# A two-layer decoder on one core: the five written orders of its steps are permuted

## The reference

```python
x = _layernorm(x + _L0_attn_ref(x, q, k, v, o))         # linear attention, 16 heads of 16
x = _layernorm(x + _L0_xattn_ref(x, ids, ctx))          # 4 experts over ctx, chosen by token id
x = _layernorm(x + _L0_ffn_ref(x, Wg, Wu, Wd, Wr))      # 8 gated experts, "golden" weights
x = _layernorm(x + _L1_attn_ref(x, Wq, Wk, Wv))         # softmax in groups of 32 tokens, half the heads rolled
x = _layernorm(x + _L1_xattn_ref(x, ctx, mask))         # attention over ctx with a pad mask
x = _layernorm(x + _L1_ffn_ref(x, gate, gate_up, down)) # 8 experts, top 2, and a shared one
```

## Time and profile before

| | us |
|---|---|
| median of 3 runs | 436.18 |
| lowest, highest | 435.44, 438.01 |
| the profiled execution | 438.25 |
| its span | 436.3 |
| TensorE (PE) busy | 417.6 |
| POOL, DVE, ACT busy | 275.3, 260.0, 242.8 |
| mean granted TensorE clock | 0.989 |

### The profile page before, as it was taken

How to read it: one execution, slowest core, us unless ns; L and a number is a source line. 1 busy time by engine, 2 the same in 40 slices (tenths; PEclk the granted TensorE clock), 3 DMA queues, 4 the chain that set the end, 5 groups by cost and what they waited for, 6 DMA issues and landing times.

```text
span 436.3 us, 9331 instructions
## 1 busy us (share of the span) xinstructions
PE 417.6 (96%) x3638; PEld 363.4 (83%) x3638; DVE 260.0 (60%) x634; ACT 242.8 (56%) x422; POOL 275.3 (63%) x237
## 2 busy tenths in 40 slices
...
GB/s 254 190 113 142 38 2 0 2 73 50 72 78 125 115 47 122 30 119 95 84 78 74 38 2 108 93 43 62 171 78 79 125 99 74 159 156 147 134 34 98
DMA packets 19335, 39.28 MB, mean 90 GB/s; under 512 B 2731, under 2 KB 6827, under 8 KB 19292
## 3 DMA queue, kind: packets, MB, share of 16 engines
...
q10 hardware_dynamic: 476, 0.60, 0.5%
...
## 4 chain that ended last, share of the span: by engine, by line
PE 82%; DVE 10%; issue 2%; ACT 2%; DMA 1%; POOL 1%; DVEq 0%; POOLq 0%; ACTq 0%
PE bank L485 14%; PE bank L488 13%; PE bank L486 13%; PE bank L730 8%; PE bank L732 8%; PE bank L731 8%; PE bank L806 2%; PE bank L749 2%; DVE hraw L1576 1%; DVE sil L1560 1%; PE bank L794 1%; DMA q_buf<-x_cols_dram 1%; PE bank L508 1%; PE bank L780 1%; PE bank L779 1%
## 5 line engine op out<-in xcount | busy, mean ns | idle before, releaser
L1269 POOL TENSOR_TENSOR h_lo<-hraw,h_hi 128x512 fp32r<-128x512 f32 x76 | 99.8, 1316 | 79.6 <-ACT h_hi L1059 79.6
L485 PE MATMUL bank<-xT_hi,pk_hi 128*128 128x512 f32 x256 | 103.9, 406 | 1.1 <-DVE hraw L1576 1.1
L486 PE MATMUL bank<-xT_hi,pk_lo 128*128 128x512 f32 x256 | 101.9, 398 | 0.0
L1059 ACT ACTIVATE h_hi<-hraw 128x512 fp32r<-128x512 f32 x76 | 47.8, 629 | 78.8 <-DVE hraw L1576 76.8
L1576 DVE TENSOR_TENSOR hraw<-bank,sil 128x512 f32<-128x512 f32 x76 | 52.4, 690 | 53.3 <-ACT sil L1047 24.6
L488 PE MATMUL bank<-xT_lo,pk_hi 128*128 128x512 f32 x256 | 81.4, 399 | 1.0 <-issue 1.0
L730 PE MATMUL bank<-pk_hi,h_hi 128*128 128x256 f32 x272 | 77.8, 286 | 1.3 <-POOL h_lo L1269 1.0
L732 PE MATMUL bank<-pk_hi,h_lo 128*128 128x256 f32 x272 | 76.8, 283 | 0.0
L731 PE MATMUL bank<-pk_lo,h_hi 128*128 128x256 f32 x272 | 76.8, 282 | 0.0
L1275 POOL TENSOR_TENSOR pk_lo<-pk_raw,pk_hi 128x512 fp32r<-128x512 f32 (+1 forms) x44 | 74.9, 1703 | 2.7 <-ACT pk_hi L1077 2.5
L485 PEld LDWEIGHTS bank<-xT_hi,pk_hi 128*128 128x128 f32 x256 | 48.7, 190 | 13.1 <-DVE hraw L1576 2.7
...
## 6 DMA issues: line engine op xcount, KB each, us to landing
...
```

What stands on the lines that cost most here:

```text
L485: pe.matmul(o, w(kc)[0], x(kc)[0], start=kc == 0, stop=False)
L486: pe.matmul(o, w(kc)[1], x(kc)[0], start=False, stop=False)
L1059: A(h_hi[:, row, at * 512:(at + 1) * 512], hraw[:, s % 2, :], ACT.Copy).then_inc(sems["hid_hi"], 1)
L1269: pool.tensor_tensor(h_lo[:, row, q], hraw[:, s % 2, :], h_hi[:, row, q].bitcast(F32), ALU.subtract).then_inc(sems["hid_lo"], 1)
```

## The change

Every list keeps exactly its steps; only their order changes. The diff is the five strings. Its core, as far as the prediction speaks of it (lines shortened to the places that differ):

```diff
 PE_ORDER
-b0.3 b1.0 b0.4 b0.5 b0.6 b0.7 b1.1 b0.8 b1.2 b0.9 b1.3
+b0.3 b0.4 b0.5 b0.6 b0.7 b1.0 b0.8 b1.1 b0.9 b1.2 b1.3
...
-r1.2 d11 r1.3 d12 g26 ... u31 d14 d15 g32 u32 g33 u33 g34 e0.12 e1.12 u34 g35 u35 a0.3 d16 a0.4 g36 u36 g37 a0.5 a0.6
+d11 u26 g27 r1.2 ... u31 r1.3 d14 d15 g32 u32 g33 u33 e0.12 e1.12 g34 u34 g35 u35 a0.3 g36 a0.4 d16 u36 a0.5 a0.6 g37
...
-u48 g49 e2.12 e3.12 u49 g50 a0.24 a1.3 a1.4 u50 d24 a1.5 a1.6 a1.7 g51 a1.8 u51 g52 u52 d25 d26 d27 a1.10 g53 u53 a1.25 g54 u54 a1.11
+u48 g49 u49 e2.12 e3.12 g50 u50 a0.24 a1.3 a1.4 d24 d25 a1.5 a1.6 a1.7 d26 a1.8 g51 u51 g52 u52 g53 u53 a1.10 d27 a1.25 g54 u54 a1.11
 ACT_ORDER
-p0 p1 p2 p3 b0.0 b0.1 b0.2 b0.3 b1.0 p4 X0 X1 X2 X3 b1.1 b0.8
+p0 p1 b0.0 b0.1 b0.2 b0.3 p2 p3 p4 X0 X1 b1.0 b0.8 X2 X3 b1.1
...
-S4 G19 D19 G20 D20 G21 s51 h51 a1.9 s52 D21 G22 D22 G23 D23 h52
+S4 h50 D20 G21 D21 s51 G22 D22 a1.9 h51 s52 G23 D23 h52
 POOL_ORDER
-G8 D8 G9 e0.10 e1.10 v0 l32 l33 D9 S1 G10 D10 l34
+D8 G9 e0.10 e1.10 D9 G10 S1 l32 l33 D10 G11 l34
...
-S4 G19 D19 G20 a1.7 a1.8 l51 D20 G21 D21 G22 D22 G23 D23 l52
+S4 l50 D20 G21 D21 a1.7 a1.8 G22 D22 l51 G23 D23 l52
 DVE_ORDER
-m32 r1.5 m33 e0.12 e1.12 m34 c a0.3 a16 a0.4
+m32 r1.5 m33 e0.12 e1.12 c a0.3 a0.4 m34 a16
...
-o52 m52 a1.10 a1.25 o53 m53 o54 m54 a1.11
+o52 m52 a1.10 o53 m53 o54 m54 a1.25 a1.11
 SP_ORDER
-G21 W0 C3 C4 S4 G22 C5 G23 G24 C6 G25 G26 R2 C7 C8 C9 R3 G27
+W0 S4 G21 C3 C4 G22 G23 G24 C5 G25 C6 G26 C7 C8 R2 C9 R3 C10 G27
```

More of the change, by code:

```diff
@@ L125 @@
 SP_ORDER = """
-G0 D0 G1 D1 S0 G2 D2 G3 D3 G4 D4 G5 D5 G6 S1 D6 G7 D7 G8 D8 G9 D9 G10 D10 G11 D11 S2 G12 D12 S3 G13 D13 G14 D14 G15 R0
-D15 R1 G16 G17 G18 G19 G20 G21 W0 C3 C4 S4 G22 C5 G23 G24 C6 G25 G26 R2 C7 C8 C9 R3 G27 C10 G28 G29 C11 C12 G30 C13
-G31 G32 G33 G34 W1 G35 C17 C18 G36 C19 C20 G37 G38 G39 C21 G40 C22 G41 C23 C24 G42 C25 G43 C26 C27 O0
+G0 D0 G1 D1 S0 G2 D2 G3 D3 G4 D4 G5 D5 G6 D6 G7 S1 D7 G8 D8 G9 D9 G10 D10 G11 D11 G12 S2 D12 G13 S3 D13 G14 D14 G15 R0
+D15 R1 G16 G17 G18 G19 G20 W0 S4 G21 C3 C4 G22 G23 G24 C5 G25 C6 G26 C7 C8 R2 C9 R3 C10 G27 G28 G29 C11 G30 C12 G31
@@ L129 @@
+G32 C13 G33 G34 W1 G35 C17 C18 G36 G37 C19 G38 C20 C21 C22 G39 G40 G41 C23 C24 G42 G43 C25 C26 C27 O0
 """.split()
 PE_ORDER = """
[L131 to L139, removed]
```

65 lines of the change are left out of this document (37 added, 28 removed).

## The result

The changed kernel is slower: 440.32 us median (440.14 to 442.99, 5 runs) against 436.24 (435.44 to 438.01, 5 runs), ratio 1.0098 [1.0067, 1.0129]. Measured again it was 441.49 against 435.51, 1.0150 [1.0101, 1.0200]. The prediction was 435.3 us with a range up to 438.5: wrong in sign.

The account below looks back on a forecast made before the run. TensorE, busy 417.6 of 436.3 us, was taken as the bound, so only its holes could change. Terms 0.3 + 0 - 0.1 - 0.85 - 0.2 + 0 = -0.85 us, taken from the median 436.18, gave 435.3 us; range 431.7 to 438.5.

Parts of the forecast that it names:

- Part 3: 160 to 190 us: m33 0.9 us earlier, hole before a0.4 0.8 us larger; net -0.1 us, bounds -1.5 to +2.4.
- Part 1: Head, 15 to 40 us: new holes before b0.4 to b0.6, the one before b0.9 goes; net +0.3 us.
- Part 2: 42 to 160 us: u and d steps swap places within one or two; 0, bounds -0.1 to +1.5 us.
- Part 4: 262 to 286 us: u49 ahead covers the holes at e2.12 and e3.12; -0.85 us, bounds -1.0 to +0.6.
- Part 5: Values steps, 306 to 321 us: instruction-block stops move and shorten, slow clock kept; -0.2 us, bounds -2.8 to +0.6.
- rival B: Second stop near 1.5 us, so TensorE's clock stays up and does not fall to 1.2 GHz; 432.2 us, chance 0.29.
- Rival C: Slower: late instruction blocks lengthen the stops, slow clock on full work, a VectorE-GpSimd collision (+1); 438.7 us, chance 0.18.
- D: Rival: the order does not act, all new positions lie within slack; 0 change, 436.2 us, chance 0.15.

Follow-up runs that it names:

- the second profile: The kernel before, unedited, profiled once more: span 434.6 us, runs 434.47 to 439.87 us.

## Why the prediction was wrong, by its steps

**Part 3 is the step that failed.** It gave -0.1 us, with bounds of -1.5 to +2.4, and took m33 0.9 us earlier. m33 came 1.9 us later; start to start the stretch costs 2.4 us in the traces from g35 to the end of u36, 2.0 us from g32 to a0.5, and 1.4 to 4.5 us by the times. The term for the wait before a0.4, 0.8 us more, was right (0.83 became 1.74 at full clock); the 0.9 us that the earlier m33 was to give is what turned round. The two rows needed were shown: an instruction of 0.17 us takes 0.90 when GpSimd is at work, and D9 and G10 would run where r1.5 runs. The prediction named the collision, priced it at up to 2.4 us, and chose the other end, on the ground that L1617 and L1404 would be free. They were; but the chain has some thirty tiny instructions one behind the other, and taking GpSimd off one of them brings another under it. The price is what is left of GpSimd's instruction (up to 1.3 and 2.34 us), not the length of VectorE's.

The sentence on SBUF — State Buffer (SBUF: two separate sides) of the Trainium skill called the collisions certain and this part +2. By that rule the trace agrees: 1.28 and 2.07 us, each ending within 0.04 us of GpSimd's. The rows of before already bore it out, and the choice should have been its side.

**Part 1** had the right holes and the wrong size for one. It gave 0.2, 0.35 and 0.6 us; measured 0.24, 0.37 and 1.60. The third was taken against TensorE's arrival in the one execution profiled, where the clock rose at 10.6 us. In 15 of the 17 profiles of all kernels it rose between 4.6 and 7.7 us. Then TensorE comes 1.8 us earlier, and the masked state, set by ACT, VectorE and GpSimd, only 0.8: predicted for 20.95 us, it was there at 20.16. The hole before b0.9 went as said (0.75). Net +1.45 for +0.3.

**Part 2** gave 0 with bounds to +1.5: u21 lost 1.0 us, which the times hardly show.

**Part 4** was right: -0.9 us for -0.85 at e2.12 and e3.12, in all profiles with that move.

**Part 5** was right on the places (after 10 instructions of d27, and the 121st matmul of a1.25) and on the sizes of the stops (1.27 and 1.62 us for 1.35 and 2.1). It was wrong in its base: 6.7 us of loss stood there in the execution profiled, but in the second profile the second stop was 0.8 us and the slow clock 3.4 us shorter. The prediction set the whole profile 2.07 us above the median and carried its largest loss over undiminished; there was less to win.

**The sum and the range.** The terms add up as stated, but the range of 431.7 to 438.5 doesn't go from B's centre to C's, as the text has it: those are 432.2 and 438.7. The measured time lies above C's centre.

**The slow clock** was treated as one event at 315 us, with rival B (it goes) at 0.29. What came was its multiplication. Behind a wait of u35 of 2.7 to 3.0 us the clock fell in four of six profiles; where that wait was 1.15 us or less, in none. It fell in d23 in five of nine profiles with after's order around it and in none of eight with before's. Why d23 draws it, with 0.34 us idle ahead, is open; on TensorE the order differs there only in d21 standing behind u47. Of u35's loss none is clock: from u35 to a0.5 it takes 14.75, 14.74 and 14.76 us in three profiles with 1.2 GHz there, and 14.75 and 14.77 in two with full clock, as TensorE's next wait is shorter by as much where the clock is slow. In d23 its 1.5 us stay to the end. So the two new slow stretches together added 1.5 us to the profile of after.

**Rival C** came true in its outcome (slower, 438.7), but not by its mechanism, which was late blocks; its +1 for the collision was the part that counted. **D** fell.

That the two stretches are the cause is shown: with both as before the time is before's; with the second alone put into before, it is slower by a ratio of 1.0115. How the 4.1 to 6.0 us divide between them isn't: alone, the head is worth 2.5 us in after and 0.6 in before, the second stretch 1.4 in after and 4.5 in before. Each of these has an interval of 1.5 us or more to either side, and the 4.5 holds a seam's wait of 1.23 us; in after the two sum to 3.9, near the whole. Whether they add up is not shown either way.

The best that the experiments point to, the kernel before with u49 moved and d27 or g54 between the dense steps, is 0.2 to 0.4% under before: at the edge of what can be measured.
